# Deferred projections and folds, conv taps by DMA, and an earlier feed-forward chain in a chained attention kernel

## What is computed

```
x  -> L0: group norm, 8-head attention over 1024 tokens, projection, + x
   -> L1: group norm, + position table                        = x1
          spatial weights: 1x1 conv 256->32, silu, 3x3 conv 32->32, silu, 1x1 conv ->1, sigmoid
          group norm(x1) -> 8-head attention                  = "1"
          two 128-wide heads, queries from x1 * spatial weights = "m"
          silu([1, m] W1 + b1) W2 + b2, then out projection, group norm, + L1's input
   -> L2: group norm, 8-head attention, projection, + normed input
   -> L3: group norm, 1-head attention (256 wide), projection, + input
```

## Time and profile before

| | us |
|---|---|
| median of 3 runs | 5167.28 |
| lowest and highest | 5163.3 and 5195.27 |
| the profiled execution | 5180.53 |
| its span, first to last instruction | 5178.8 |
| mean granted TensorE clock in it | 0.952 |

### The profile page before, as it was taken

How to read it: one execution, slowest core, us unless ns; L and a number is a source line. 1 busy time by engine, 2 the same in 40 slices (tenths; PEclk the granted TensorE clock), 3 DMA queues, 4 the chain that set the end, 5 groups by cost and what they waited for, 6 DMA issues and landing times. The chain is left out here.

```text
span 5178.8 us, 62450 instructions
## 1 busy us (share of the span) xinstructions
PE 4859.7 (94%) x21680; PEld 2237.7 (43%) x21680; DVE 3050.9 (59%) x5432; ACT 2408.6 (47%) x4321; POOL 3061.1 (59%) x1733
## 2 busy tenths in 40 slices
PE   7789999999999999999999999999999999999887
PEld 3325334553335533364334643346334453345434
DVE  6455677366673666646765467655676456773462
ACT  3352555435553355524555245552555425553251
POOL 3472777447764477635877368663677537774361
PEclk8899899998899999999999999899999999999999
DMA  3111212021110221102210112201122022110110
GB/s 89 28 35 47 55 38 56 21 56 46 47 43 21 62 57 41 34 29 65 56 44 20 41 50 58 50 13 47 46 56 56 7 62 54 44 45 11 30 37 13
DMA packets 103605, 221.16 MB, mean 43 GB/s; under 512 B 31104, under 2 KB 33408, under 8 KB 103168
## 3 DMA queue, kind: packets, MB, share of 16 engines
q1 hardware_dynamic: 103296, 217.16, 16.3%
HBM read 56.47 MB, written 8.39 MB: 13 GB/s over the span
## 5 line engine op out<-in xcount | busy, mean ns | idle before, releaser
L881 ACT ACTIVATE probs<-bank 128x512 f32<-128x512 f32 x3456 | 1929.2, 599 | 2312.6 <-PE bank L543 2279.7
L984 DVE TENSOR_REDUCE max_cols<-bank 128x1 f32<-128x512 f32 x3456 | 2188.6, 682 | 1261.3 <-PE bank L543 1254.0
L1231 POOL TENSOR_TENSOR probs_added<-probs_added,probs 128x1024 f32<-128x1024 f32 x852 | 1991.3, 2375 | 48.7 <-ACT probs L881 48.4
L543 PE MATMUL bank<-q_stack,k_stack 97*128 97x512 f32 (+1 forms) x3584 | 1664.3, 520 | 64.1 <-DVE max_cols L984 31.3
L543 PE MATMUL bank<-probs,v_tokens 128*32 128x512 f32 (+1 forms) x7168 | 1366.0, 635 | 13.1 <-ACT probs L881 12.9
L1231 POOL TENSOR_TENSOR probs_added<-probs 128x1024 f32<-128x1024 f32 x192 | 453.5, 2368 | 934.8 <-ACT probs L881 933.1
L543 PEld LDWEIGHTS bank<-q_stack,k_stack 97*128 97x128 f32 (+1 forms) x3584 | 665.1, 195 | 760.1 <-issue 408.9
L543 PE MATMUL bank<-act,weight_stream 128*128 128x512 f32 x1792 | 925.5, 618 | 20.4 <-ACT probs L881 7.2
L1218 POOL TENSOR_TENSOR probs_added<-probs_added,probs 128x512 f32<-128x512 f32 x288 | 368.1, 1278 | 624.0 <-ACT probs L881 622.8
L543 PE MATMUL bank<-high_parts 32*128 32x512 f32 x3072 | 405.2, 515 | 99.6 <-DVE max_cols L984 84.7
L543 PEld LDWEIGHTS bank<-probs,v_tokens 128*32 128x32 f32 (+1 forms) x7168 | 316.4, 121 | 415.6 <-issue 280.8
(11 more groups left out here) (84 smaller groups left out, 2923.4 us busy)
## 6 DMA issues: line engine op xcount, KB each, us to landing
k_stack<-high_parts SPq DMA_DIRECT2D x384, 128.0 KB, 2.4
q_stack<-high_parts SPq DMA_DIRECT2D x768, 64.0 KB, 2.0
weight_stream<-stream_dram SPq DMA_DIRECT2D x32, 768.0 KB, 4.3
k_stack<-low_parts SPq DMA_DIRECT2D x192, 128.0 KB, 2.4
q_stack<-low_parts SPq DMA_DIRECT2D x384, 64.0 KB, 2.0
act<-x_dram SPq DMA_DIRECT2D x8, 1024.0 KB, 6.5
act<-pos_dram SPq DMA_DIRECT2D x8, 1024.0 KB, 5.8
weight_stream<-stream_dram SPq DMA_DIRECT2D x16, 512.0 KB, 3.9
```

The costliest lines, as they stand in the source:

```text
L543: return nc.tensor.matmul(dst, lhsT, rhs, start=start, stop=stop, **kw)
L881: act.activation(PR[:, PLACE[m], j, :], bank[:, :], ACT.Exp, scale=att.scale).then_inc(reading(key), 1)
L984: dve.tensor_reduce(cols[:, kh, j, qt:qt + 1], bank[:, :], AX.X, ALU.max).then_inc(reading(key), 1)
L1231: pool.tensor_tensor(ADD[:, js, :], one, two, ALU.add).then_inc(p_added, 1)
```

## The change

Four things:

1. In an attention without a host that follows an unhosted `Between` of kind 0, 1 or 2 (`alone`), the projections of `group(1)` move from ahead of the attention to its units 2 to 10. Three places.
2. The folded products move from ahead of the plan into the first attention (units 34, 38, 42), and `FOLDED` from `PR`'s place into activation buffers 3 and 4.
3. "sa1 mix" writes the middle shift alone; SP copies it to the two other groups of 32 partitions, one column left and right, and "sa2" waits for all four copies of the sample.
4. In `stages("2")` feed-forward products, statistics, the norm "post", the residual and the norm "2" get other units, and step 1 of a hosting attention 0 adds six items on GpSimd, not seven.

```diff
     def beside(self, between):
-        for s in {"0": range(4), "2": (1, 2)}.get(self.kind, ()) if between is not None else ():
+        for s in {"0": (0, 2, 3), "2": (1, 2)}.get(self.kind, ()) if between is not None else ():
             self.added[s] = ADDED_BESIDE
...
     elif kind == "2":
         out = []
-        for n, (nh, m) in enumerate((nh, m) for nh in range(NH) for m in range(CT)):
-            out += unit("ff1", (nh, m), 4, 2.1 + 5 * n, 1.2)
-        for n, (nh, m) in enumerate((nh, m) for nh in range(NH) for m in range(CT)):
-            out += tile("ffo", (nh, m), 2, 24.9 + 2.4 * n, 1.2)
-            out.append((28.3 + 2.4 * n, "stats", ("o", m, nh)))
-        out += norm("post", 36.8, 2.5, "o", "o") + each("res", QUARTERS, 49, 1.2) + \
-            each("stats", [("x",) + q for q in QUARTERS], 55, 1.5) + norm("2", 61.5, 2.5, "x", "m") + \
+        halves = [(nh, m) for nh in range(NH) for m in range(CT)]
+        for i, at in zip(halves, (2.1, 6.7, 11.3, 17.6)):
+            out += unit("ff1", i, 4, at, 1.2)
+        for i, at in zip(halves, (15.9, 22.6, 25.7, 28.1)):
+            out += tile("ffo", i, 2, at, 1.2)
+            out.append((at + 3.2, "stats", ("o",) + i[::-1]))
+        out += norm("post", 33.3, 2.5, "o", "o") + each("res", QUARTERS, 45.8, 1.2) + \
+            each("stats", [("x",) + q for q in QUARTERS], 53, 1.5) + norm("2", 59.5, 2.3, "x", "m") + \
             projections(group(0), 78.6, 1) + stacks(87, 1.8) + values(88.6, 1.9) + projections(group(1), 110.1, 1.6) + \
             narrow_start(87, 121.5, 118, 4)
...
+    if alone:
+        out = [e for e in out if not (e[1][0] in "qk" and e[1][1:] in ("", " out", " low") and
+                                      (e[2][0] if e[1][1:] else e[2][0][0]) == 1)]
...
+            between.alone = att is None and between.kind in "012" and (between.feeds, None) in slots
...
     for att, between in SLOTS:
-        left = stages(between.kind) if between is not None else []
+        left, beside = [], between
+        if between is not None:
+            left = stages(between.kind, between.alone)
+        elif last is not None and last.alone:
+            left, beside = projections(group(1), 2, 1), last
+            if att is ATTS[0]:
+                left += [(34 + 4 * i, "fold", i) for i in range(3)]
+            left.sort(key=lambda e: e[0])
+        last = between
...
-        FOLDED = sb("fold_in", [P, FOLD_COLS], at=pr_at)
+        FOLDED = sb("fold_in", [P, FOLD_COLS], at=buf_at + 3 * CT * T * 4)
...
                     if part == 0:
                         until_read(pe, ("sa1", it.sample, 1))
+                        pe.wait_ge(shifted, 64 * (it.sample + 1))
...
-                    for j in range(3):
-                        r = slice(D * j, D * j + D)
-                        v, u = (x.rearrange("p (r c) -> p r c", c=SIDE)
-                                for x in (bank[r, :], act_buf(it.turn, "f")[r, 1, half(i)]))
-                        ins = dve.scalar_tensor_tensor(
-                            out=padded_image(it.turn)[r, 1 + rows * i:1 + rows * (i + 1), 2 - j:2 - j + SIDE],
-                            in0=v, scalar=wcol("bsa1", 0, D, D * j), in1=u, op0=ALU.add, op1=ALU.mult)
-                    ins.then_inc(reading(key), 1)
+                    r = slice(D, 2 * D)
+                    v, u = (x.rearrange("p (r c) -> p r c", c=SIDE)
+                            for x in (bank[r, :], act_buf(it.turn, "f")[r, 1, half(i)]))
+                    dve.scalar_tensor_tensor(
+                        out=padded_image(it.turn)[r, 1 + rows * i:1 + rows * (i + 1), 1:1 + SIDE],
+                        in0=v, scalar=wcol("bsa1", 0, D, D), in1=u, op0=ALU.add, op1=ALU.mult)\
+                       .then_inc(reading(key), 1)
...
+                elif event == "sa1 mix":
+                    until_read(sp, ("sa1", it.sample, i))
+                    image, n = flat_image(it.turn), EDGE * SIDE // NH
+                    at = EDGE + n * i
+                    for j in (0, 2):
+                        to = at + 1 - j
+                        sp.dma_start(image[D * j:D * j + D, to:to + n], image[D:2 * D, at:at + n])\
+                          .then_inc(shifted, 16)
```

More of the change, by code:

```diff
@@ L99, in __init__ @@
         self.kind, self.turn, self.sample = kind, turn, sample
+        self.alone = False
 QUARTERS = [(t, nh) for nh in range(NH) for t in range(CT)]
@@ L176, in narrow_start, with stages @@
         quads([(1, n) for n in range(EARLY_QUADS)], early, step, min(0.45, step / GROUP))
-def stages(kind):
+def stages(kind, alone=False):
     if kind == "0":
@@ L281, in plan @@
 def plan():
-    behind = None
+    behind, last = None, None
     for att, between in SLOTS:
-        left = stages(between.kind) if between is not None else []
+        left, beside = [], between
[7 more added lines that the diff above has]
+        last = between
         if att is None:
@@ L291, in plan @@
             for _, name, i in left:
-                yield name, between, i
+                yield name, beside, i
         else:
@@ L422, in build_program @@
         HALVED = sb("halved_bias", [P, 5])
+        buf_at = base[0]
         BUF = [sb(f"act{i}", [P, CT, T]) for i in range(6)]
@@ L488, in build_program, with flat_image @@
         EDGE = SIDE + 2
+        def flat_image(turn):
+            return act_buf(turn, "o")[0:3 * D, :, :].rearrange("p a b -> p (a b)")[:, 0:EDGE * EDGE]
         def padded_image(turn):
[L491 to L492 removed]
+            return flat_image(turn).rearrange("p (r c) -> p r c", c=EDGE)
         def wide_part(kind, o, part):
@@ L750, in folding, with fold @@
                 return FOLDED[:, a:a + n].rearrange("p (k n) -> p k n", n=C)
-            for i, (first, second) in enumerate((("ff2", "ffo"), ("wv3", "wp3"))):
+            def fold(i):
                 bank = take(("fold", i))
-                for m in range(CT):
-                    for k in range(CT):
-                        ins = mm(bank[:, m * C:(m + 1) * C], folding(first)[:, k, m * P:(m + 1) * P],
-                                 folding(second)[:, k, :], k == 0, k == CT - 1)
-                ins.then_inc(filling(("fold", i)), 1)
-            bank = take(("fold", 2))
-            for i, (name, bias) in enumerate((("wp0", "bv0"), ("wp2", "bv2"), ("wp3", "bv3"), ("ffo", "bff2"))):
-                for m in range(CT):
-                    for k in range(CT):
-                        c = CT * i + m
-                        ins = mm(bank[:, c:c + 1], folding(name)[:, k, m * P:(m + 1) * P], wcol(bias, k), k == 0,
-                                 k == CT - 1)
-            ins.then_inc(filling(("fold", 2)), 1)
+                if i < 2:
+                    first, second = (("ff2", "ffo"), ("wv3", "wp3"))[i]
+                    if i == 0:
+                        pe.wait_ge(fold_loaded, 16)
+                    for m in range(CT):
+                        for k in range(CT):
+                            ins = mm(bank[:, m * C:(m + 1) * C], folding(first)[:, k, m * P:(m + 1) * P],
+                                     folding(second)[:, k, :], k == 0, k == CT - 1)
+                else:
+                    for n, (name, bias) in enumerate((("wp0", "bv0"), ("wp2", "bv2"), ("wp3", "bv3"), ("ffo", "bff2"))):
+                        for m in range(CT):
+                            for k in range(CT):
+                                c = CT * n + m
+                                ins = mm(bank[:, c:c + 1], folding(name)[:, k, m * P:(m + 1) * P], wcol(bias, k),
+                                         k == 0, k == CT - 1)
+                ins.then_inc(filling(("fold", i)), 1)
             for event, it, i in PLAN:
@@ L772, in _ @@
                     rest(it, i)
+                elif event == "fold":
+                    fold(i)
                 elif event == "mean":
@@ L1056, in rest, with fold @@
                     columns(att, s)
-            for i, (dst, factor) in enumerate(((FF, 0.5), (WV3, 1.0))):
+            def fold(i):
                 bank = until_full(dve, ("fold", i))
-                dve.tensor_scalar(dst[:, :], bank[:, :], factor, None, ALU.mult).then_inc(reading(("fold", i)), 1)
+                if i < 2:
+                    dst, factor = ((FF, 0.5), (WV3, 1.0))[i]
+                    ins = dve.tensor_scalar(dst[:, :], bank[:, :], factor, None, ALU.mult)
+                else:
+                    for n, name in enumerate(("bp0", "bp2", "bp3", "bffo")):
+                        ins = dve.tensor_tensor(BOUT[:, n, :], bank[:, CT * n:CT * n + CT], w(name), ALU.add)
+                ins.then_inc(reading(("fold", i)), 1)
             a, _ = AT["sa2"]
@@ L1068, in _ @@
             after("halved")
-            bank = until_full(dve, ("fold", 2))
-            for i, name in enumerate(("bp0", "bp2", "bp3", "bffo")):
-                ins = dve.tensor_tensor(BOUT[:, i, :], bank[:, CT * i:CT * i + CT], w(name), ALU.add)
-            ins.then_inc(reading(("fold", 2)), 1)
```

(1 more changed line is left out.)

4 lines of the change are left out of this document (1 added, 3 removed).

## The result

| | before | after |
|---|---|---|
| median, us | 5171.07 (4 runs) | 5112.05 (4 runs, 5108.67 to 5115.33) |
| ratio | | 0.9887, 95% interval 0.986 to 0.9914 |
| span of the profiled execution | 5178.8 | 5113.5 |
| mean granted clock in it | 0.952 | 0.963 |

A forecast was written before the change was run, and what follows sets the result against it. TensorE was taken as the bound, busy 4859.7 of 5178.8 us; terms -8 - 4 - 11 + 1 - 20 + 0.5 - 37 = -78.5 gave 5102 profiled, median 5088 us, range 5060 to 5115.

The forecast's parts named there:

- Start, folds, second group: Program start and three unhosted attentions: earlier statistics and first scores, less work paid inside attentions; -8 and -4 us.
- Taps, the waits: Attention 2's convolution: VectorE loses four of six mix steps per sample, so TensorE waits less; -11 us over seven.
- Rival C: Tap copies arrive late: "sa2" waits 2 us in each of 8 samples, the clock gains nothing; 5142 us, chance 0.08.
- Taps, the clock: Hosted attentions 2: fewer waits mean less time at the low clock, 0.33 us gained per us; some 16 us.
- 7 of 24 [us less] in attention 2: Each hosted attention 2 was to lose 7 of its about 24 us at the low clock.
- Feed-forward: Seven hosting attentions 0: moved statistics, residual, norms and six GpSimd items save 2.9 us each; -20 us.
- the -1.4 "of the 1.48 us stall": Attention 0, unit 63: VectorE's 1.48 us stall behind a GpSimd residual add was to shrink by 1.4 us.
- The clock in attention 0: Hosting attentions 0: fewer waits in units 36 to 67 mean less low clock, at 0.33 us per us.
- 9 of 22: Each hosting attention 0 was to lose 9 of its about 22 us at the low clock.
- Rival A: Waits go but the clock stays, as its dips belong to the lean units 35 to 79; 5126 us, chance 0.25.
- Rival B: The clock comes back wholly in the hosted attentions 0 and 2; 5020 us, chance 0.10.
- Rival D: Feed-forward matmuls end earlier in attention 0, the lean stretch grows, all at low clock; slower, 5211 us, chance 0.07.

The follow-up runs named there:

- taps-only run: The kernel before with the neighbour taps copied by DMA and nothing else changed: 5114.65 us against 5176.39, ratio 0.9895.
- the doses put back: Kernel before with DMA taps, the removed VectorE mixes of both halves put back with old operands, writing a scratch tile: 5172.37 us against 5175.96, ratio 0.9997.
- late-norm kernel: The changed kernel with feed-forward's statistics of x and the norm behind them 2 units later: 5058.41 us against 5168.65 for the kernel before, ratio 0.9785.
- the runs above: For 58 and 133 us low: the late-norm kernel, 5058.41 us, and the same with the residual adds at 49 instead of 45.8, 5083.3 us.

## Why the prediction was right, and where it was not

About the whole gain came from the taps, which I had at 27 of 79 us (waits and clock) and which gave 54 to 62, and the largest term, feed-forward with its clock at 41, gave nothing alone and cost some 8 us beside the rest. The total was near because these two misses, some 30 us one way and 40 to 50 the other, nearly cancelled. That was luck.

**Start, folds, second group.** Right. The steps added up to -11.4 at the ends (the rounded sum has -10.5), measured -8.1: -19.2 ahead of the first attention (the step said 14.7 + 6 = 20.7), -7.8 ahead of sample 7's attention 2 (8.9 less 0.5), and prices inside the attentions of 3.9 and 4.7 where I had 6. The stretch that holds the folds and sample 0's convolution grew by 8.5 where the steps give 5.7, and the m of sample 0 by 1.7 where I had none.

**Taps, the waits.** Right. The step gave -11; the taps-only run lost 12.8 us of idle time in the seven attentions 2. The copy was as estimated from q_stack, 2.0 us to land, and "sa2" did not wait. The page's DMA issues, then sample 3's convolution:

```profile
act<-act SPq DMA_DIRECT2D x32, 68.0 KB, 2.0
```

```profile
1954.28 5.26 SPq L1396 DMA_DIRECT2D act<-act  x4
...
1955.34 0.51 PE L564 MATMUL bank<-high_parts 32*128 32x512 f32 x4
...
1957.64 0.74 DVE L1185 SCALAR_TENSOR_TENSOR act<-bank,weights,act 32x512 f32<-32x512 f32 x1
...
1959.36 0.51 PE L564 MATMUL bank<-high_parts 32*128 32x512 f32 x4 [0.21 <-DVE max_cols L1011]
...
1961.10 1.02 PE L564 MATMUL bank<-act,weights 96*32 96x512 f32 x2
```

The 1.21 us of the earlier trace rows are gone, 0.21 is left behind the second mix, "sa2" starts 2.7 us after that mix ended, at 1961.10. The last copy was issued at about 1959.0 and landed at about 1961.0, so by this estimate the cover is thin: 0.1 us. Rival C did not happen.

**Taps, the clock.** The failed step is "7 of 24 [us less] in attention 2". The low time fell by 17 of 24 us each (167 to 48 over seven). I had made the clock go back by about the share of the waits that went. And 0.33 us per low us, from one pair of attentions, was too little: busy time over low time is 53.3 / 119 = 0.45 for the change, 42.3 / 102 = 0.41 for the doses put back, 37.4 / 96 = 0.39 for the late norm. By the rule of the Trainium skill that the prediction weighed (TensorE: Matmul & The Clock Gate, "Terms") it is 0.5; the runs stand between the two. With 17 and 0.43 the term for attention 2 would have been 51 us, not 16.

**Feed-forward.** The failed step is the -1.4 "of the 1.48 us stall". I set GpSimd's gain of 2.3 us against VectorE asking 1.4 us earlier and took the stall for gone. GpSimd's gain came: sample 3's last residual add ends 75.1 us into the attention and not 77.5. But the stall in the kernel before stood behind the third residual add, and this kept VectorE from asking for the last one before it was there:

```profile
1848.12 0.69 DVE L1088 BATCH_NORM_STATS2 stats<-act 128x6 f32<-128x512 f32 x1
```

That is 77.5 us in. Now it asks at 1815.44, 73.6 us in: 3.9 us earlier, not 1.4. So it stalls again (1.52 us) behind the last residual add, which ends behind a 2.35 us sum, and the norm's mean product, 2 units earlier, brought the wait onto TensorE directly: 2.5 us per attention. The other steps held in part: the wait for GpSimd's sums (1.6 us) is gone, and the wait at units 36 to 39 went down from 2.1 to 1.6, half of the 1.0 forecast. One wait was not in the sum: a feed-forward product waits 0.56 us for its gate at unit 26, in the hosted attentions too. Taken together idle time rose by 2.3 us over the seven, where my waits alone (without the 1.0 us of sums that TensorE pays) gave -3.9 x 7.

**The clock in attention 0.** "9 of 22" did not come: low time 157 to 154. The idle time that was to bring it had not gone; with that mended, in the late-norm kernel, it fell to 58. So the mechanism of the forecast, that low time goes when waits go, holds in both places, and its size was set too low in both. It does not hold as a rule on the amount of idle time: the runs above have the same idle time with 58 and 133 us low, and more idle time with less. Rival A, that the clock belongs to the lean stretch and not to the waits, is refuted by the run with the old mixes put back and by the late-norm kernel, each of which changes only 1.3 and 1.6 us of idle time per attention. Rival B was nearer for attention 2 than my own choice. Rival D did not come true: the ffo products end earlier in the late-norm kernel too, and it has the least low time of all in attention 0.

## What to carry to other kernels

A wait of 1 to 2 us on TensorE in a stretch where it has little spare work can be worth several times itself where the clock goes down with it, as it did at two places of this kernel and did not at every wait: count the time at the lower level per stretch, beside idle time. Here a us of it cost 0.39 to 0.45 us of busy time. When several steps of a chain are moved forward together, look for a consumer that moved further than its producer, since it, and all that stands behind it, now waits in a place where nothing waited before; split such a change, as the good half and the bad half can hide each other wholly. A dose put back to test a cause must have the old operands as well as the old length.

## What the runs showed of the hardware

VectorE and GpSimd: a VectorE step of 32 x 512 with one source in PSUM took 0.74 us beside running GpSimd adds, the same step with two sources in SBUF 0.74 us when GpSimd was free and up to 8.2 us when it was not. The Trainium skill (SBUF — State Buffer, "Who interferes with whom") says that a VectorE instruction with two SBUF inputs contends with a GpSimd instruction that reads SBUF, and that the order of issue decides which of them is blocked. The trace agrees on who contends. How long the later one stays blocked differs here: the step at 1993.05 did not get in between two adds, with 2.33 us per add it passed two of their boundaries and began about when the fifth ended, while the one at 2004.23 got in at the first boundary. What decides between the two is not shown.

The clock: the same 705 matmul records of attention 2 took 139.94 us busy with the clock full all the time, 151.30 at a mean of 0.91 and 157.83 at 0.88, and 1.5 us of VectorE time per sample or twice that decided how often each came. Attentions with the same idle time came out at either end (7.47 and 7.39 us idle, 157.83 and 141.31 busy), so here the clock was worth more than the waits that brought it down, and less certain.
